# A four-layer block on 4096 tokens: layer-norm statistics finished inside the stages instead of in blocks between them, and a stage's weight transfers reordered

## The reference

```python
def _layernorm(x, axis=-1, eps=1e-05):
    m = jnp.mean(x, axis=axis, keepdims=True)
    v = jnp.var(x, axis=axis, keepdims=True)
    return (x - m) / jnp.sqrt(v + eps)
...
    x = x + _L0_xattn_ref(_layernorm(x, axis=-1), ctx_2048, mask_BxS2_bk0)
    x = x + _L0_ffn_ref(_layernorm(x, axis=-1), L0_ffn_gate_w, ...)
    x = x + _L1_xattn_ref(_layernorm(x, axis=-1), ctx_2048, ctx_2048, L1_xattn_Wh, ...)
    x = x + _L1_ffn_ref(_layernorm(x, axis=-1), L1_ffn_in_gamma, ...)
    x = x + _L2_xattn_ref(_layernorm(x, axis=-1), ctx_2048, itok_BxS_0_1023, L2_xattn_W_kvc, ...)
    x = x + _L2_ffn_ref(_layernorm(x, axis=-1), L2_ffn_w1, L2_ffn_w2, L2_ffn_w3)
    x = x + _L3_xattn_ref(_layernorm(x, axis=-1), ctx_2048, ctx_2048, L3_xattn_gamma)
    x = x + _L3_ffn_ref(_layernorm(x, axis=-1), L3_ffn_gate_w, ...)
    return x
```

```python
        x_norm = layer_norm(x, in_gamma, in_beta)
        thought = x_norm[:, -1, :] @ agg_w + agg_b
        for _ in range(K_STEPS):
            t = layer_norm(thought, pn_gamma, pn_beta)
            t = jax.nn.gelu(t @ d1_w + d1_b, approximate=False)
            thought = thought + (t @ d2_w + d2_b)
        broadcast = (thought @ bc_w + bc_b)[:, None, :]
        if USE_GATING:
            gate = jax.nn.sigmoid(x @ gate_w + gate_b)
            out = x + gate * broadcast
        else:
            out = x + broadcast
        return layer_norm(out, out_gamma, out_beta)
```

## Time and profile before

| | us |
| --- | --- |
| median of three runs | 2349.25 (2346.01 to 2354.24) |
| the profiled execution, its own time | 2338.15 |
| its span, first to last instruction | 2336.3 |
| mean granted TensorE clock, as a share of full speed | 0.910 |

### The profile page before, as it was taken

The page is one execution under the profiler, slowest core; times in us unless marked ns, Lnnn a source line. Parts: engine busy times, 40 slices in busy tenths (PEclk is TensorE's granted clock), DMA queues, the critical chain, the costliest instruction groups (busy, mean ns, idle before and its releaser), DMA issues. The chain is left out here.

```text
span 2336.3 us, 47384 instructions
## 1 busy us (share of the span) xinstructions
PE 1909.4 (82%) x16190; PEld 1422.9 (61%) x16190; DVE 1584.4 (68%) x3652; ACT 990.3 (42%) x2485; POOL 1185.6 (51%) x1528
## 2 busy tenths in 40 slices
PE   6979745597833988888887999499999999779995
PEld 5869522585622777777765666256666665446773
DVE  7955721567677899999983554588888885553446
ACT  3733221143233555555542222156766666533331
POOL 4620036523374666666662223268888877462331
PEclk8989857799966999999998999689999999889997
DMA  6721046502050000000000000334444441533337
GB/s 205 253 73 51 10 137 153 189 6 66 1 149 1 1 0 0 0 0 0 0 1 1 1 1 1 88 78 113 105 113 108 108 110 28 152 112 94 109 106 232
DMA packets 140322, 172.66 MB, mean 74 GB/s; under 512 B 31345, under 2 KB 121633, under 8 KB 135521
## 3 DMA queue, kind: packets, MB, share of 16 engines
q1 hardware_dynamic: 130321, 148.01, 22.9%
q0 software_dynamic: 9808, 22.23, 3.2%
HBM read 117.59 MB, written 52.00 MB: 73 GB/s over the span
## 5 line engine op out<-in xcount | busy, mean ns | idle before, releaser
L2702 DVE TENSOR_REDUCE mx<-bank 128x2 f32<-128x512 f32 x512 | 321.2, 680 | 84.2 <-PE bank L2564 83.8
L2668 ACT ACTIVATE e<-bank 128x512 f32<-128x512 f32 x512 | 269.0, 607 | 130.6 <-PE bank L2584 130.6
L2496 POOL TENSOR_TENSOR es<-e 128x256 f32<-128x256 f32 x384 | 271.2, 728 | 85.8 <-ACT e L2668 85.3
L2564 PE MATMUL bank<-k,q 72*128 72x256 bf16 x1024 | 204.1, 284 | 33.5 <-DMA k<-k_parts 33.3
L1849 POOL TENSOR_TENSOR q_l<-q_l,rot_l 64x512 f32<-64x512 f32 x128 | 162.3, 1268 | 129.7 <-DVE rot_l L2046 129.7
L2584 PE MATMUL bank<-q,k 74*128 74x256 bf16 x1024 | 195.4, 274 | 5.2 <-DMA q<-rows 2.8
L2564 PEld LDWEIGHTS bank<-k,q 72*128 72x128 bf16 x1024 | 91.9, 100 | 94.9 <-issue 48.2
L2601 PE MATMUL bank<-e,val 128*32 128x256 f32 x2048 | 138.8, 389 | 3.1 <-ACT nd L2663 0.6
L2894 POOL DMA_INDIRECT y<-y,y_row x71 | 68.7, 968 | 125.1 <-DVE y L3171 122.1
L1881 PE MATMUL bank<-qcT,wq_abs 96*128 96x128 f32 x1024 | 126.1, 283 | 0.0
L1881 PEld LDWEIGHTS bank<-qcT,wq_abs 96*128 96x128 f32 x1024 | 120.3, 197 | 2.6 <-issue 0.2
(11 more groups left out here) (445 smaller groups left out, 5138.0 us busy)
## 6 DMA issues: line engine op xcount, KB each, us to landing
q<-q_parts SPq DMA_DIRECT2D x32, 576.0 KB
k<-k_parts SPq DMA_DIRECT2D x96, 192.0 KB
got<-rows SPq DMA_DIRECT2D x71, 129.0 KB, 2.2
moe_rows<-zero_a SPq DMA_DIRECT2D x16, 512.0 KB, 3.2
w<-in_e0w SPq DMA_DIRECT2D x16, 512.0 KB, 3.7
parts_y<-y SPq DMA_DIRECT2D x32, 256.0 KB, 4.5
k_parts<-k_parts_a SPq DMA_DIRECT2D x96, 64.0 KB, 2.0
q_parts<-parts SPq DMA_DIRECT2D x96, 64.0 KB, 2.0
```

The lines of the kernel that those rows point to most:

```text
L2496: nc.gpsimd.tensor_tensor(es[:, n, :], e[:, n, 0, :], e[:, n, 1, :], ALU.add).then_inc(s["sum_ready"], 1)
L2564: last = nc.tensor.matmul(scores(r)[:, qt * D:(qt + 1) * D], q[0:R, b, h * D + qt * P:h * D + qt * P + P], k[0:R, b, h * D:(h + 1) * D], s ...
L2668: nc.scalar.activation(e[:, slot(i, r), :, :].rearrange("p k n -> p (k n)"), scoresT(r)[:, :], ACT.Exp).then_inc(s["exp_ready"], 1)
L2702: v.tensor_reduce(mx[:, a.n, 0, at:at + 2], scores(r)[:, :].rearrange("p (a n) -> p a n", a=2), AX.X, ALU.max, negate=True).then_inc(s["ma ...
```

## The change

`finish_stats` is no block any more but 18 instructions inside a stage's DVE program, made for a slice of the columns. The 28 columns `EARLY` are finished in the stage that makes them, ahead of its last additions; the four columns `LATE4` near the beginning of the next. Both are made at all six places. The memset of `minus_half` stands once, at the beginning of layer 0 attention, on POOL. In layer 2 attention ACT, and in think SP, wait for LATE4 (`stats_done`) before an instruction that needs or overwrites what it uses. In layer 2 and layer 3 attention DVE waits for an event of its last tile before EARLY (`sum_ready`, `rec_ready`). In think SP issues its transfers in the order of their use, in groups that have their own semaphores, and PE, ACT and DVE wait for each group where they use it. DVE takes the two norms of the last tokens before the first bias additions.

```diff
-def finish_stats(nc, c, tag, eps=LN_EPS, shift=None):
-
-    with ExitStack() as ctx:
-        s = open_sems(nc, ctx, f"{tag}_chain {tag}_half_set")
-        block = ctx.enter_context(nc.Block())
-
-        @block.vector
-        def _(dve):
-            ch = Chain(dve, s[f"{tag}_chain"])
-            newton_rstd(nc, c, ch.link, c.bn, c.mean, c.rstd, slice(0, NT), eps)
-            if shift is not None:
-                nc.vector.scalar_tensor_tensor(out=shift, in0=c.mean[:, :], scalar=-1.0, in1=c.rstd[:, :],
-                                               op0=ALU.mult, op1=ALU.mult)
-
-        @block.gpsimd
-        def _(pool):
-            nc.gpsimd.memset(c.minus_half[:, :], -0.5).then_inc(s[f"{tag}_half_set"], 1)
+EARLY, LATE4 = slice(0, NT - 4), slice(NT - 4, NT)
+
+
+def finish_stats(nc, c, ch, cols, shift=None):
+
+    newton_rstd(nc, c, ch.link, c.bn, c.mean, c.rstd, cols, LN_EPS)
+    if shift is not None:
+        ch.link(nc.vector.scalar_tensor_tensor(out=shift[:, cols], in0=c.mean[:, cols], scalar=-1.0, in1=c.rstd[:, cols],
+                                               op0=ALU.mult, op1=ALU.mult))
...
+            nc.gpsimd.memset(c.minus_half[:, :], -0.5).then_inc(s["half_set"], 1)
...
             def add(t):
+                if t == NT - 3:
+                    finish_stats(nc, c, sch, EARLY)
...
             norm(0)
             norm(1)
+            finish_stats(nc, c, Chain(dve, s["stat_chain"]), LATE4)
...
             for n in range(PAIRS + 4):
...
                 if n >= 4:
                     add(n - 4)
+                if n == PAIRS + 1:
+                    finish_stats(nc, c, sch, EARLY)
...
+            rows = lambda name: sp.dma_start(row[name][:, :], c.d["f1_" + name].broadcast_to([M, D]))
+            by_rows = lambda name: c.d["f1_" + name].rearrange("(k p) n -> p k n", p=P)
+            sp.dma_start(gw[:, :, :], by_rows("gate_w")).then_inc(s["g_weights"], 16)
             for b in range(2):
                 sp.dma_start(last_x[32 * b:32 * b + 32, :], c.x[64 * b + 63:64 * b + 64, :, :]).then_inc(s["t_last"], 16)
-            sp.dma_start(gw[:, :, :], c.d["f1_gate_w"].rearrange("(k p) n -> p k n", p=P)).then_inc(s["g_weights"], 16)
-            sp.dma_start(wide["gate_b"][:, :], c.d["f1_gate_b"].broadcast_to([P, D])).then_inc(s["g_weights"], 16)
+            for name in ("in_gamma", "in_beta"):
+                rows(name).then_inc(s["t_in"], 16)
+            sp.dma_start(wide["gate_b"][:, :], c.d["f1_gate_b"].broadcast_to([P, D])).then_inc(s["g_bias"], 16)
+            sp.dma_start(agg[:, :, :], by_rows("agg_w")).then_inc(s["t_agg"], 16)
+            rows("agg_b").then_inc(s["t_agg"], 16)
+            sp.dma_start(d1[:, :, :], by_rows("d1_w")).then_inc(s["t_loaded"], 16)
+            for name in ("pn_gamma", "pn_beta"):
+                rows(name).then_inc(s["t_loaded"], 16)
+            sp.dma_start(d1b[:, :], c.d["f1_d1_b"]).then_inc(s["t_loaded"], 16)
+            sp.dma_start(d2[:, :, :], by_rows("d2_w")).then_inc(s["t_loaded"], 16)
+            rows("d2_b").then_inc(s["t_loaded"], 16)
+            sp.dma_start(bcw[:, :, :], by_rows("bc_w")).then_inc(s["t_loaded"], 16)
+            rows("bc_b").then_inc(s["t_loaded"], 16)
+            sp.wait_ge(s["stats_done"], 1)
             sp.dma_start(c.seg_i, c.d["seg"]).then_inc(s["seg_loaded"], 16)
-            for name, dst in row.items():
-                sp.dma_start(dst[:, :], c.d["f1_" + name].broadcast_to([M, D])).then_inc(s["t_loaded"], 16)
-            for dst, name in ((agg, "agg_w"), (d1, "d1_w"), (d2, "d2_w"), (bcw, "bc_w")):
-                sp.dma_start(dst[:, :, :], c.d["f1_" + name].rearrange("(k p) n -> p k n", p=P)).then_inc(s["t_loaded"], 16)
-            sp.dma_start(d1b[:, :], c.d["f1_d1_b"]).then_inc(s["t_loaded"], 16)
             for name in ("out_gamma", "out_beta"):
...
-            pe.wait_ge(s["g_weights"], 32)
+            pe.wait_ge(s["g_weights"], 16)
             tiles(0)
-            pe.wait_ge(s["t_loaded"], 16 * (5 + len(row)))
...
+                if n == 0:
+                    pe.wait_ge(s["t_agg"], 32)
+                if n == 1:
+                    pe.wait_ge(s["t_loaded"], 128)
...
-            act.wait_ge(s["t_loaded"], 16 * (5 + len(row)))
...
+                    act.wait_ge(s["t_loaded"], 128)
...
             features(0)
             features(1)
-            dve.wait_ge(s["g_weights"], 32)
+            sch = Chain(dve, s["stat_chain"])
+            finish_stats(nc, c, sch, LATE4)
+            dve.sem_inc(s["stats_done"], 1)
+            dve.wait_ge(s["t_last"], 32)
+            norm(0, last_x, LN_EPS)
+            dve.wait_ge(s["t_in"], 32)
+            norm(1, n1, EPS1, row["in_gamma"], row["in_beta"])
+            dve.wait_ge(s["g_bias"], 16)
             biased(0)
-            dve.wait_ge(s["t_last"], 32)
-            dve.wait_ge(s["t_loaded"], 16 * (5 + len(row)))
-            norm(0, last_x, LN_EPS)
-            norm(1, n1, EPS1, row["in_gamma"], row["in_beta"])
             features(2)
             biased(1)
+            dve.wait_ge(s["t_agg"], 32)
             dve.wait_ge(s["t_down"], 1)
             v.tensor_tensor(th[:, :], c.bank[1][0:M, 0:D], row["agg_b"][:, :], ALU.add).then_inc(s["t_added"], 1)
+            dve.wait_ge(s["t_loaded"], 128)
...
             for g in range(GR + 1):
                 if g < GR:
                     front(g)
+                if g == GR:
+                    finish_stats(nc, c, sch, EARLY, c.shift)
                 if g >= 1:
                     back(g - 1)
...
             compress(1)
+            act.wait_ge(s["stats_done"], 1)
             nope(0, 0)
...
+            sch = Chain(dve, s["stat_chain"])
+            finish_stats(nc, c, sch, LATE4, c.shift)
+            dve.sem_inc(s["stats_done"], 1)
             rope(0, 0)
...
             softened(NT - 1, 1)
+            dve.wait_ge(s["sum_ready"], halves(NT - 1, 1))
+            finish_stats(nc, c, sch, EARLY)
             back(NT - 1, 1)
...
                 x_rest(1, 1)
+                finish_stats(nc, c, sch, LATE4)
                 hidden(0, 0)
...
             def step_before_last(t, j):
                 hidden_rest(t, j)
                 hidden(t + 1, 1 - j)
+                finish_stats(nc, c, sch, EARLY)
                 add(t, j)
...
+            sch = Chain(dve, s["stat_chain"])
+            finish_stats(nc, c, sch, LATE4)
             v.tensor_scalar(c.rstd[:, :], c.rstd[:, :], float(np.float32(DQ3) ** np.float32(-0.5)), None,
...
             run(dve, tile)
             end = At(NT // BUF - 1, BUF - 1)
+            dve.wait_ge(s["rec_ready"], tile_ready(end.t) - 1)
+            finish_stats(nc, c, sch, EARLY)
             invert(end)
             stats(end.to(-1))
             stats(end)
...
+            finish_stats(nc, c, Chain(dve, s["stat_chain"]), LATE4)
             norms(2)
...
-        finish_stats(nc, c, "st5")
...
-            finish_stats(nc, c, "st1")
...
-        finish_stats(nc, c, "st3")
...
+            c.shift = res("shift_l", [P, NT])
             stage_l1_think(nc, c)
             recycle(nc)
-            c.shift = res("shift_l", [P, NT])
-            finish_stats(nc, c, "st4", shift=c.shift[:, :])
...
-    finish_stats(nc, c, "st6")
     stage_l3_attention(nc, c)
-    finish_stats(nc, c, "st7")
```

32 lines of the change are left out of this document (20 added, 12 removed).

## The result

The changed kernel takes 2335.27 us (median of 5 runs, 2332.68 to 2338.33) against 2349.25 us before (5 runs, 2346.01 to 2354.24): ratio 0.9938, 95% interval 0.9921 to 0.9956, so 14.0 us less where 22.3 were forecast. It lies in the range and in the direction of the forecast, at 63% of its size. On another chip (experiment e2) the ratio was 0.9928 (0.9900 to 0.9955), 17.1 us.

The account below looks back on a forecast made before the run. TensorE is busy 82%, DVE 68%, but at six seams only DVE works; 4.2 + 8.0 + 3.3 + 4.2 - 1.6 + 4.2 = 22.3 us off the median 2349.25 gives 2326.95, range 2314 to 2338.

Parts of the forecast that it names:

- Seam 4: Layer 2 attention to ternary: both chains fall into DVE idles of 8.88 and 6.80, whole block gained, +4.2 us.
- seam 6: Layer 3 attention to moe: chains fall into DVE idles of 8.10 and 7.64, whole block gained, +4.2 us.
- seam 1: Layer 0 attention to ffn: both chains covered, stage's end SP's by 1 us or more, whole block gained, +4.2 us.
- Rival C: LATE4 exposed in the heads of seams 1, 3, 4 and 6: 12.6 us less, gain 9.7; chance 0.09.
- Rival D: Slower: the two chains cost more than the block, EARLY on the path too; -6.1 us, time 2355.4; chance 0.05.
- Rival B: TensorE's clock gains as well at ternary's head, idle about 2 keeping 2.4 GHz: at most 5.0 us more; chance 0.05.
- seam 2: Mix to think: block 4.2, less 1.5 for EARLY, plus 5.3 from think's new order, +8.0 us.
- seam 3: Think to layer 2 attention: block 4.2, less 0.9 for EARLY, LATE4's wait costed at nothing, +3.3 us.
- Think: Think's head, new order: first transpose of thoughts 20 us after the first normalize, not 25.3; gain 5.3, bounds 4.0 and 6.2.
- Rival A: The gain in think stays away: 5.3 us less, gain 17.0, time 2332.2; chance 0.10.
- Seam 5's head: Start of layer 3 attention: LATE4 exposed ahead of the scaling, -3.15 us; whole seam -1.6, bounds -2 and -0.7.
- Seam 5's tail: End of ternary: EARLY delays the last tile's hrest_t, which POOL and PE wait for; tail 2.6 us longer.

Follow-up runs that it names:

- e2: The changed kernel, unchanged, timed again on another chip with a second profile; ratio to before 0.9928.
- e3: The changed kernel with the think of before, to which only the two chains are added; ratio to before 0.9942.
- e1: The kernel before, unchanged, run on another chip for a second profile; 2379.4 us.
- e4: The kernel before, with its blocks, given only the new think without its chains; ratio to before 0.9965.
- e11: e8 with the chains at the ends of layer 2 and 3 attention and the heads of ternary and moe made twice; ratio to before 0.9916.
- e10: e8 with 31 small chained instructions, result unused, ahead of the scaling at layer 3 attention's head; that stage took 518.04 us.
- e7: The changed kernel with layer 3 attention's four-column chain moved behind its first four norms; ratio to before 0.9913.
- e8: The changed kernel with both moves, e6's in ternary's tail and e7's in layer 3 attention's head; ratio to before 0.9891.
- e9: e8 with 8 small chained instructions, result unused, ahead of the scaling at layer 3 attention's head; that stage took 515.31 us.
- e5: The changed kernel with the statistics between ternary and layer 3 attention back in a block on all 32 columns; ratio to before 0.9919.
- e6: The changed kernel with the 28-column chain at ternary's end moved behind the last hidden_rest; ratio to before 0.9916.

## Why the prediction was right, and where it was off

**The blocks are worth 4.2 each, and a covered chain nothing: right.** Seam 4 gained 4.7. The timeline of the changed kernel there:

```profile
1223.89 0.21 DVE L194 TENSOR_TENSOR mean_all<-bn_all 128x28 f32<-128x28 f32 x1
...
1232.76 0.42 DVE L2093 TENSOR_TENSOR x_all<-bank,x_all 128x256 f32<-128x256 f32 x1 [4.42 <-PE bank L1932]
...
1234.19 0.74 DVE L223 TENSOR_SCALAR xn_t<-x_all,mean_all,rstd_all 128x256 f32<-128x256 f32 x2 [0.35 <-POOLq L166]
...
1237.69 0.57 DVE L194 TENSOR_TENSOR mean_all<-bn_all 128x4 f32<-128x4 f32 x1
...
1244.98 0.95 DVE L2313 TENSOR_TENSOR sig_t<-bank,sig_t 128x512 f32<-128x512 f32 x2 [3.29 <-ACT sig_t L2269]
```

EARLY stands in the idle that was 8.88, of which 4.42 are left, and LATE4 ahead of `hidden(0, 0)`, of whose 6.80 3.29 are left. At seam 6 the chain is covered only just: it takes 6.9 us beside POOL's work, and of the idle of 8.10 ahead of the last reciprocal 1.28 is left; 7.64 became 5.71, with moe 1.4 us longer than before in the first pair of profiles and 0.4 shorter in the mean of e2 and e3 against e1 and e4. The timeline of the changed kernel at the end of layer 3 attention, POOL and VectorE:

```profile
1979.62 4.98 POOL L2532 TENSOR_TENSOR es<-e 128x256 f32<-128x256 f32 x7 [0.41 <-ACT e L2704]
...
1980.87 0.24 DVE L194 TENSOR_TENSOR mean_all<-bn_all 128x28 f32<-128x28 f32 x1
...
1983.32 0.64 DVE L201 TENSOR_SCALAR small<-small 128x28 f32<-128x28 f32 x1
...
1987.56 0.19 DVE L207 SCALAR_TENSOR_TENSOR rstd_all<-small,rstd_all 128x28 f32<-128x28 f32 x1
...
1989.02 1.75 DVE L2744 RECIPROCAL rec<-nd 128x256 f32<-128x256 f32 x1 [1.28 <-ACT nd L2699]
```

At seam 1 it is as close. VectorE's timeline in the kernel before, the statistics of tile 28:

```profile
131.60 0.43 DVE L525 BATCH_NORM_STATS2 bn_all<-x_all 128x6 f32<-128x256 f32 x1
```

and in the changed kernel those of tile 28, those of tile 31 and the first work of the next stage:

```profile
135.22 0.43 DVE L522 BATCH_NORM_STATS2 bn_all<-x_all 128x6 f32<-128x256 f32 x1
...
146.68 0.43 DVE L522 BATCH_NORM_STATS2 bn_all<-x_all 128x6 f32<-128x256 f32 x1
147.41 0.94 DVE L223 TENSOR_SCALAR xn_b<-x_all,mean_all,rstd_all 128x256 f32<-128x256 f32 x2 [0.31 <-PEq L249]
```

From tile 28's statistics, the last ahead of the chain, to the next stage it is 16.3 us in the three profiles with the block and 11.9 to 12.4 in the eleven without: 3.9 to 4.4 gained for a forecast of 4.2. But the stage's end is now VectorE's, 0.3 behind its last statistics, in all eleven; the prediction had it as SP's by 1 us or more, and nothing of that room is left. The 1.4 that the table's row misses lies ahead of the chain, where tile 28's statistics themselves come 1.3 later in the mean (130.3 to 135.2 against 130.6 to 132.0).

Rival C falls with this: LATE4 is not exposed in the heads of seams 4 and 6, and even twice the chain costs nothing at seam 4 and little at seam 6 (e11). Rival D had no place left to come from. Rival B is out by the clock's rows: TensorE's idle ahead of ternary is 2.0 in all eleven, as it supposed, and yet the granted clock falls within 2 us of the stage's start and is back 8.1 to 8.8 us into it, where it was back after 7.5 to 8.1 before (in the changed kernel 0.51 from 1235.4 to 1242.3).

**EARLY at 3.6: too low where POOL works.** In mix the chain took 4.7. The timeline of the changed kernel, VectorE and POOL:

```profile
559.00 0.21 DVE L194 TENSOR_TENSOR mean_all<-bn_all 128x28 f32<-128x28 f32 x1
559.12 1.28 DVE L195 TENSOR_TENSOR small<-bn_all 128x28 f32<-128x28 f32 x1
560.32 0.20 DVE L196 TENSOR_TENSOR small<-bn_all 128x28 f32<-128x28 f32 x1
...
563.72 0.69 DVE L1419 TENSOR_TENSOR x_all<-bank,x_all 128x512 f32<-128x512 f32 x1
...
559.02 1.32 POOL L1325 TENSOR_TENSOR yT_m<-yT_m,gate 128x512 f32<-128x512 f32 x1 [0.29 <-ACT yT_m L1384]
```

The second instruction takes 1.28 where its neighbours take 0.2; it ends at 560.40, just behind POOL's TENSOR_TENSOR of 1.32, which ends at 560.34. At the end of layer 0 attention the chain took 136.08 to 141.30, 5.2 us (4.9 to 5.4 in the eleven profiles), before the last group in think 5.7 with its shift, at the end of layer 2 attention 4.5 and of layer 3 attention 6.9, with POOL at work in all of them. Only in ternary, ahead of tile 30's addition, it took the 3.6. The Trainium skill ("SBUF - State Buffer", section "SBUF: two separate sides") has a VectorE instruction with two SBUF inputs and a GpSimd instruction that reads SBUF exclude each other for a whole instruction; the row of 1.28 agrees. At the end of layer 3 attention instructions with one input, like the TENSOR_SCALAR at 1983.32, take 0.6 as well. The chain's length was taken from rows in which POOL stood still. It costs what it is longer wherever it is on the path. At seam 2, from the start of the third-last addition to think it is 11.0 us in the three profiles with the block and 9.4 in all eleven others: 1.7 gained and not 2.7, which is this 1.1. At seam 3, from the end of VectorE's last instruction ahead of the chain to ACT's first work in layer 2 attention it is 14.0 and 12.5: 1.5 gained and not 3.3, for a chain of 5.7 put at 3.8. The stage of mix as a whole gains 1.7 in five profiles (63.3 to 63.5) and nothing in six (65.0 to 65.5): there the clock was low for longer, until 13 us into the stage and not until 9 or 10, or not at all, long before the chain, which then can't be its cause. What the cause is stays open.

**Think: the right mechanism, and 20 for 18.9 to 23.0.** Rival A does not hold: e4 alone is 8.3 us less, and with both halves the first transpose comes 2 to 7 us sooner in every profile. In the mean it comes at 21.3, so the gain is 4.5 for 5.3. The spread is the clock's, as the prediction said, but its bounds, 19.1 and 21.3, were too narrow: seven of nine profiles lie outside. Where the clock is up 9.3 us into the stage and stays up in the head the transpose comes at 18.9 (e2, e10), where after 14 to 16 us at 20.5 (e7, e8), where after 16 to 17 at 21.5 to 23.0 (the rest). The sum behind these bounds has a slip as well: four tiles of 1.1 behind 10.5 end at 14.9 and not at 15.4. The steps behind add to the spread: a fall of the clock in one of the four costs about 3 us in some profiles and not in others, before and after.

**Seam 5's head: the step that failed.** The prediction has "LATE4 is the first work of the next stage, ahead of the scaling that all wait for: -3.15". The order was read rightly and the price was not: the stage is 9.7 us longer than in the seven profiles without the chain (516.6 against 506.9). The rows split it. (1) The first maxima come 4.1 later in the mean: 3.15 of chain, and about 1 because the transfers behind it land later after their issue. (2) By the 60th they are 6.3 later: TensorE stays longer at 1.2 GHz, and its wait for `q<-rows` is 2.1 to 6.3 and not 0.2 to 3.4. (3) The rest, 3.4, is gathered over the 400 us behind. Cut into slices of 5 us, each worth its length times what the clock lacks to 1, this part of the stage loses 3.4 to 6.9 us to short falls of the clock in the four profiles with the chain (4.8 in the mean; 5.1 and 3.4 in e9 and e10) and 0 to 3.4 in the seven without (1.5). TensorE waits for a transfer of `k` four to nine times on the way in all of them, nearly always for 0.6 to 1.4 us; why the clock falls more often where the head was late is open. This split is one of means and no account of single profiles: in the four with the chain the 60th maxima come at 72.4 to 79.7 us into the stage, e3's nearly as early as e5's 72.1 without it, and yet the four stages are equally long within 0.8 us. That the delay at the head is the cause is shown (e5, e7, e9, e10); by which way it becomes 9.7 is shown for some 6 of them in the mean and argued for the rest. The prediction's bounds for this seam, -2 and -0.7, took the delay as the same at the end as at the beginning; behind the head TensorE is busy for 97% of the time (423.45 of 438 us), so the delay is not made up, and here it grew.

**Seam 5's tail: right,** 2.75 for 2.6, and so is what followed from it: the idle stood behind the row and not ahead of it, and moving the chain there gave 3.0 back (e6). The other bound of this seam, +0.9 from filling the idle ahead of the memset of `k`, gave nothing: the idle is still 0.91.

**The sum.** Of the forecast 22.3 the profiles' means miss 13.1: 7.4 in layer 3 attention, 2.1 in mix, 1.4, 1.6 and 1.1 in layer 0 attention, think and ternary, less 0.5 in layer 2 attention. By cause it is some 7 for the delay at seam 5's head, 2.8 for the longer chains at seams 2 and 3, and for the rest the clock and the scatter of layer 0 attention. The timed runs miss 8.3 and 5.2. 2335.27 lies in the range on record, which was widened for the rivals, and 1.3 above the 2319 to 2334 of the forecast's own case: the cause is none of the rivals, but the size of one term above all. That it lies in the wider range owes something to luck: the bounds of seam 5 alone, -2 and -0.7, leave out the -8.2 that came of it (4.2 - 2.7 - 9.7), and room made for rivals that did not come took it in.

## What to carry to other kernels

Work that moves out of a block between stages is free only where its engine waits ahead of the row that others wait for; read for each place which side of the late row the idle is on. A delay at the head of a long stage that TensorE fills can be worth more than its own length, here three times as much and five times for the shortest: the transfers behind it land later and the clock comes up later, so put nothing ahead of the first work that feeds a store. Take a chain's duration from rows in which the same neighbours run, POOL above all, and compare stages over several profiles before a difference of a few us is given a cause.

## What was not expected of the hardware

- A chain instruction of 28 columns on VectorE took 1.28 us and not 0.2 beside POOL's TENSOR_TENSOR of 1.32 us, and 18 of them 4.5 to 6.9 and not 3.6.
- The granted clock comes up 50 to 55 us into layer 3 attention without a chain at its head and 54 to 63 us into it with one, though the chain is 3.15 us.
- The same code of the thinking stage took 162.1 to 171.2 us from profile to profile, a step of its serial work 12.7 to 13.5 us or about 3 more, with a stretch at the lower clock. Ternary with the tail moved has two lengths, 239.0 and 240.6, the longer with one more fall of the clock, and mix with the chain 63.3 to 63.5 and 65.0 to 65.5; in mix the longer one goes with a lower clock from 10 to 15 us into the stage (0.65 to 0.73 there, against 1.00).
